# One convolution pair in every slot, the first six in the slots of the image two ahead, in a two-layer convolution kernel

## The chip, the cores and the metric

The kernel runs on one core of one Trainium2 chip. The metric is the device time of the whole program in microseconds (us), the median of several executions. PE is TensorE, DVE is VectorE, ACT is ScalarE, POOL is GpSimd, SP is SyncE, which here only issues DMAs.

## The reference

The input x has 32 images of 16 channels and 256 x 256 points, in fp32. Two residual layers follow each other, each with a group normalisation (8 groups of 2 channels) ahead of it:

```
x = x + conv3x3_int8(group_norm(x))          # layer 0
x = x + irfft2(conv3x3_complex(rfft2(group_norm(x))))   # layer 1
```

Layer 0 scales the normalised input by the largest absolute value of the *whole* batch over 128, rounds it, clips it to +-127, convolves it with 16 x 16 x 3 x 3 integer weights, scales back and adds a bias. Layer 1 takes a real 2-D FFT, convolves the spectrum with complex 3 x 3 weights, adds a complex bias, and transforms back.

## The kernel before

A first pass reads all images and takes the statistics of the first normalisation and the batch's maximum. Then comes the main part, image by image. An image stands in SBUF as 128 partitions (16 channels by 8 rows) by 32 row blocks by 256 columns, in one of two buffers: `img[u]`, u the image's parity. Its 32 row blocks are 16 *pairs*.

**The order of the work is written out by hand.** Every engine has a function `period`, which runs for one image s and goes through 16 *slots*, t = 0 to 15. In slot t the engines finish pair t of image s, and do earlier stages of later pairs. `periods` (line 308) calls `period` for all images, with three flags: `mix` (image s is being finished), `conv` (image s + 1 is in layer 0), `ahead` (there is an image s + 2). What belongs to which slot:

- **PE** (`period`, line 1079): `turn_pair(t+4)` transposes the folded rows (L963), `dft_pair(t+3)` transforms them (L972), `mix_pair(t+1)` multiplies with the weights (L985, 48 matmuls), `finish_pair(t)` transforms back (L999 to L1004). Beside these it has layer 0 of image s + 1: `conv_pair` (three matmuls on the quantised rows, L1017, and one on the halo rows, L1019) and `row_means` of the pair before (L1030). `CONV_OF` (line 38) says which convolution pairs are in which slot: one in slots 0 to 3, two in slots 4 to 9 (the second one behind `mix_pair`), none in slots 10 to 15. Slot 10 has `group_stat` twice (L1046), for mean and variance of the second normalisation of image s + 1; slots 12 to 15 have small steps with its row means (`centre_rows`, `dft_rows`, `mix_rows`, `finish_rows`).
- **DVE** (line 905), in this order: `y_low(t)` (L827), `stats_mean` in slot 10 (L855, L857), `stats_out` in slot 11 (to L877), `x_low(t+3)` (L821), `layer0_pair` (the residual add L834 and its statistics L836), `stats_var` in slot 10 (L864 to L870), `round_pair` (L813, L815), `layer0_pair` of a second pair, `finish_pair(t)` (four adds, L844 to L849).
- **ACT** (line 564): `turn_out(t+4)` (L540), `x_high(t+3)` (L547), `scale_pair` (L533), `y_high(t+1)` (L554), and the store of pair t - 2 (L562).
- **POOL**: `fold(t+4)` (L729 to L732), which from slot 12 on is that of image s + 1 and needs its statistics.
- **SP** (line 457): in slot t it waits for the store of pair t - 3 and loads that pair of image s + 2 (`load_pair`, L376), waits for `x_low(t+3)` and the mixing of pair t + 1 and copies the result into shifted rows for PE (`restack`, L454, four DMAs), and in slots 2, 6, 10 and 14 copies halo rows of a quarter image out of the quantised rows (`halo_rows`, L443, two DMAs).

`AHEAD` = 10 says how far `scale_pair` and `round_pair` are ahead: in slot t they have pair t + 10 of image s + 1, from slot 6 on pair t - 6 of image s + 2 (`quant_of`, line 304). A convolution pair waits for the rounding of its whole quarter image (four pairs) and for the halo copies of it. `conv_ps`, where the convolution goes, has one buffer: `conv_pair` waits until DVE has added the pair before (`x1_s`).

```
dve.wait_ge(conv_s, m + 1 + PAIRS)
nc.vector.scalar_tensor_tensor(rows, conv_ps[:], out_scale, rows, ALU.mult, ALU.add).then_inc(x1_s, 1)
```

Ahead of the first image, ACT and DVE scale and round ten pairs of image 0, SP copies two quarters of halos, and one period with s = -1 runs the whole of layer 0 of image 0 (the *lead-in*).

## Time and profile before

| | |
|---|---|
| median of 3 runs | 3781.86 us (3779.63 to 3790.49) |
| the profiled execution | 3767.42 us |
| its span, first to last instruction | 3765.6 us |
| mean granted PE clock in it | 0.992 |
| images 0 to 29, 696.36 to 3604.45 us of the span | 2908.09 us, 96.94 each |
| period of image 30 | 93.91 us |

A period is counted from the first transposes of its slot 0 on PE to those of the next one. PE's matmuls overlap, so a row's duration is longer than the distance to the next row's start; distances between starts are what PE needs.

### The profile page before, as it was taken

The numbers are of one execution on the slowest core, as the hardware profiler recorded it, in microseconds if no ns is written. First come the engines' busy times: TensorE is split into PE (matmuls) and PEld (weight loads), VectorE is DVE, ScalarE is ACT, GpSimd is POOL, SyncE is SP. The second block draws the span as 40 slices with busy tenths as digits, with TensorE's granted clock in tenths as the row PEclk, the third lists the DMA queues.
The fourth block names the chain that finished last, engine by engine and source line by source line (L and its number), as shares of the span: only waits on it lengthen the run. The fifth ranks groups of instructions, "written<-read, shape, count | busy, mean of one in ns | idle before, by whom it ended". The sixth has DMA issues, their size and how long they took to land.

```text
span 3765.6 us, 126495 instructions
## 1 busy us (share of the span) xinstructions
PE 2979.5 (79%) x45732; PEld 2646.9 (70%) x45732; DVE 3117.7 (83%) x5880; ACT 1893.1 (50%) x2799; POOL 1490.4 (40%) x1984
## 2 busy tenths in 40 slices
PE   0000004899999999999999989999999999999998
PEld 0000002788888888888888878888888888888888
DVE  8999994688878888888888878888888888888876
ACT  8999981344444444444444434444444444444443
POOL 4777000344334344343343334333433433333444
PEclk9999999999999999999999999999999999999999
DMA  8767650366666666666666656666666666666655
GB/s 309 241 236 242 236 188 16 118 196 198 198 188 196 197 195 197 194 192 195 199 194 191 195 178 194 194 192 195 192 194 191 196 192 194 193 199 191 198 179 179
DMA packets 630696, 730.98 MB, mean 194 GB/s; under 512 B 76752, under 2 KB 602160, under 8 KB 614736
## 3 DMA queue, kind: packets, MB, share of 16 engines
q1 hardware_dynamic: 482640, 588.71, 48.6%
q10 hardware_dynamic: 147456, 134.28, 12.7%
q8 instruction: 374, 6.13, 0.7%
q14 instruction: 226, 1.85, 0.2%
HBM read 262.58 MB, written 134.22 MB: 105 GB/s over the span
## 4 chain that ended last, share of the span: by engine, by line
PE 50%; SPq 16%; issue 11%; DMA 11%; DVE 9%; ACT 1%; POOL 1%; ACTq 1%; DVEq 0%; POOLq 0%
PE y_ps L985 12%; PE mean_b L1030 10%; SPq L454 9%; PE conv_ps L1017 7%; PE x_ps L972 6%; DMA stack<-xn 5%; PE fin_ps L1004 5%; SPq L376 4%; PE t_ps L963 3%; DMA out<-img 3%; PE conv_ps L1019 3%; DVE scaled L758 2%; DMA img<-in_x 2%; PE fin_ps L999 2%; DVE scaled L759 1%
## 5 line engine op out<-in xcount | busy, mean ns | idle before, releaser
L729 POOL TENSOR_SCALAR eo<-img,norm 128x256 f32<-128x256 f32 x512 | 481.5, 940 | 1502.1 <-PE t_ps L963 1274.2
L985 PEld LDWEIGHTS y_ps<-mix_w,stack 128*128 128x128 f16 x24576 | 787.5, 99 | 158.1 <-DMA stack<-xn 84.6
L985 PE MATMUL y_ps<-mix_w,stack 128*128 128x64 f16 x24576 | 810.4, 194 | 62.4 <-DMA stack<-xn 62.0
L540 ACT ACTIVATE xt<-t_ps 128x512 f32<-128x512 f32 x512 | 305.8, 597 | 910.8 <-PE t_ps L963 802.9
L554 ACT ACTIVATE y_hi<-y_ps 128x512 f16<-128x512 f32 x512 | 305.8, 597 | 535.4 <-PE y_ps L985 534.4
L834 DVE SCALAR_TENSOR_TENSOR img<-conv_ps,cst,img 128x512 f32<-128x512 f32 x512 | 382.3, 747 | 226.9 <-PE conv_ps L1019 226.4
L821 DVE SCALAR_TENSOR_TENSOR xn<-x_ps,norm,xn 128x512 f16<-128x512 f32 x512 | 383.1, 748 | 220.7 <-ACT xn L547 215.6
L1030 PE MATMUL mean_b<-row_mean,img 128*128 128x48 f32 x4096 | 538.2, 275 | 16.6 <-DVE img L834 16.2
L972 PE MATMUL x_ps<-dft,xt 128*128 128x128 f32 x4096 | 543.0, 276 | 0.0
L1030 PEld LDWEIGHTS mean_b<-row_mean,img 128*128 128x128 f32 x4096 | 511.3, 196 | 31.7 <-DVE img L834 31.5
L972 PEld LDWEIGHTS x_ps<-dft,xt 128*128 128x128 f32 x4096 | 499.7, 192 | 0.1
L547 ACT ACTIVATE xn<-x_ps,norm 128x512 f16<-128x512 f32 x512 | 352.4, 688 | 231.0 <-DMA stack<-xn 145.3
L533 ACT ACTIVATE scaled<-img,b,a 128x512 f32<-128x512 f32 x512 | 412.0, 805 | 106.1 <-DVE quant L813 71.1
L1004 PE MATMUL fin_ps<-inv,y_hi 128*128 128x128 f16 x4096 | 459.1, 221 | 0.0
L951 PE MATMUL misc_ps<-im_f,group 128*128 128x32 f32 x2 | 0.6, 396 | 575.5 <-DVE im_f L779 575.5
L1017 PE MATMUL conv_ps<-quant,conv_w 128*128 128x512 bf16 x1536 | 427.2, 388 | 25.6 <-DMA halo<-quant 25.5
L951 PEld LDWEIGHTS misc_ps<-im_f,group 128*128 128x128 f32 x2 | 0.5, 310 | 575.5 <-issue 575.5
L1004 PE MATMUL fin_ps<-inv,y_lo 128*128 128x128 f16 x2048 | 400.6, 221 | 0.0
L1004 PEld LDWEIGHTS fin_ps<-inv,y_hi 128*128 128x128 f16 x4096 | 358.8, 99 | 39.6 <-issue 0.2
L730 POOL TENSOR_TENSOR eo<-img 128x256 f32<-128x256 f32 x512 | 381.1, 744 | 0.0
L732 POOL TENSOR_TENSOR eo<-eo,img 128x256 f32<-128x256 f32 x512 | 376.2, 735 | 0.0
L836 DVE BATCH_NORM_STATS2 bn<-img 128x6 f32<-128x512 f32 x512 | 355.6, 694 | 17.6
(134 smaller groups left out, 5138.9 us busy)
## 6 DMA issues: line engine op xcount, KB each, us to landing
stack<-xn SPq DMA_DIRECT2D x2048, 132.0 KB, 2.6
img<-in_x SPq DMA_DIRECT2D x1024, 128.0 KB, 2.8
out<-img ACTq DMA_DIRECT2D x1024, 128.0 KB, 3.0
img<-in_x SPq DMA_DIRECT2D x120, 1024.0 KB, 4.9
halo<-quant SPq DMA_DIRECT2D x192, 193.3 KB, 3.3
halo<-quant SPq DMA_DIRECT2D x64, 169.1 KB, 3.0
row_mean<-table_row_mean SPq DMA_DIRECT2D x1, 768.0 KB, 15.4
spread<-table_spread SPq DMA_DIRECT2D x1, 512.0 KB, 14.4
```

The source lines that it names most:

```text
L533: nc.scalar.activation(scaled[:], img[u][:, 2 * j:2 * j + 2, :], ACT.Identity, bias=b0[:, bass.ds(k, 1)], scale=a0[:, bass.ds(k, 1)]).then ...
L729: nc.gpsimd.tensor_scalar(even, rows[:, :, 0:F], norm[v][:, 2:3], None, ALU.add).then_inc(shift_s, 1)
L730: nc.gpsimd.tensor_tensor(odd, rows[:, :, 0:F], rows[:, :, N - 1:F - 1:-1], ALU.subtract)
L732: nc.gpsimd.tensor_tensor(even, even, rows[:, :, N - 1:F - 1:-1], ALU.add).then_inc(fold_s, 1)
L821: nc.vector.scalar_tensor_tensor(natural(t, 1), x_ps[:].rearrange("p q b k -> p (q b) k"), norm[v][:, 4:5], natural(t, 0), ALU.mult, ALU.s ...
L834: nc.vector.scalar_tensor_tensor(rows, conv_ps[:], out_scale, rows, ALU.mult, ALU.add).then_inc(x1_s, 1)
L836: nc.vector.bn_stats(bn[:, c, :], rows).then_inc(bn_s, 1)
L972: last = nc.tensor.matmul(x_ps[:, q, b, :], xt[:, t % 2, b, q, :], dft[:, q, :], start=True, stop=True)
L985: last = nc.tensor.matmul(y_ps[t % 2][:, g, b, :], stack[:, t % 2, g, first:first + F], mix_w[:, 2 * at + b, g, f, part, :], start=i == 0, ...
L1004: last = nc.tensor.matmul(fin_ps[:, b, q, :], y[:, t % 2, 2 * b + q].rearrange("p x g -> p (x g)"), inv[:, q, part, :], start=False, stop= ...
L1017: nc.tensor.matmul(conv_ps[:], conv0_w[:, dw, :], quant[:, 2 * c:2 * c + 2, dw:dw + N], start=dw == 0, stop=False)
L1030: nc.tensor.matmul(mean_ps[half], img[u][:, hb, F * half:F * half + F], row_mean[:, hb, :], start=False, stop=False)
```

## The change

Every slot gets one convolution pair. In slots 0 to 9 it is pair t + 6 of image s + 1, in slots 10 to 15 pair t - 10 of image s + 2. It always stands ahead of `mix_pair`; on DVE `layer0_pair` stands ahead of `stats_var` and of the rounding. Row means follow a list of their own, `MEANS_OF`: slots 14, 15 and 0 have two pairs, slots 1 to 10 one, slots 11 to 13 none, because the accumulator is in use until slot 12. Scaling and rounding are 12 pairs ahead. ACT stores pair t - 1 rather than t - 2, SP loads pair t - 2 rather than t - 3. SP's halo copies are in slots 0, 4, 8 and 12 and come first in the slot. The lead-in has no steps of its own any more: a further period with s = -2 does the first roundings and convolutions of image 0.

```diff
--- before.py
+++ after.py
@@ -35,11 +35,12 @@
 STORES = 4
 NQ = 8
 
-CONV_OF = [[j] if j < 4 else [2 * j - 4, 2 * j - 3] if j < 10 else [] for j in range(PAIRS)]
 BOUND = 5
 STATS_AT = 10
 IMAGE_AT = 12
-AHEAD = 10
+AHEAD = 12
+CONV_LEAD = 6
+MEANS_OF = {14: (0, 1), 15: (2, 3), 0: (4, 5), **{t: (t + 5,) for t in range(1, 11)}}
 TERMS = [(0, 0, 0), (0, 0, 2), (1, 0, 1), (0, 1, 1), (1, 1, 0), (1, 1, 2)]
 TABLES = ("dft", "dft_back", "channel", "ident", "inv", "row_mean", "spread", "first_row", "pulse", "group", "mask", "wave_k", "coef_m", "coef_i")
 
@@ -305,8 +306,17 @@
 
             return (1, j + AHEAD) if j < PAIRS - AHEAD else (2, j - PAIRS + AHEAD)
 
+        def conv_of(t):
+
+            return (1, t + CONV_LEAD) if t < PAIRS - CONV_LEAD else (2, t - PAIRS + CONV_LEAD)
+
+        def means_of(t):
+
+            return (2 if t >= PAIRS - 2 else 1), MEANS_OF.get(t, ())
+
         def periods(engine, period):
 
+            period(-1, 0, False, False, True)
             period(-1, 1, False, True, True)
             rounds = (SP2 - 1 - PEEL) // TURN
             for v in range(PEEL):
@@ -457,20 +467,20 @@
             def period(i, u, mix, conv, ahead):
                 s = 2 * i + u
                 for t in range(PAIRS):
-                    if mix and t >= 3 and ahead:
-                        sp.wait_ge(store_s[(t - 3) % STORES], stored(s, t - 3))
+                    if t in (0, 4) and conv:
+                        halo_rows(s + 1, t // 4 + 2)
+                    if t in (8, 12) and ahead:
+                        halo_rows(s + 2, t // 4 - 2)
+                    if mix and t >= 2 and ahead:
+                        sp.wait_ge(store_s[(t - 2) % STORES], stored(s, t - 2))
                         sp.sem_inc(tick_s, 1)
-                        load_pair(s + 2, u, t - 3)
-                    if later(s, mix) and t < 3 and conv:
-                        sp.wait_ge(store_s[(t - 3) % STORES], stored(s - 1, t + PAIRS - 3))
+                        load_pair(s + 2, u, t - 2)
+                    if later(s, mix) and t < 2 and conv:
+                        sp.wait_ge(store_s[(t - 2) % STORES], stored(s - 1, t + PAIRS - 2))
                         sp.sem_inc(tick_s, 1)
-                        load_pair(s + 1, 1 - u, t + PAIRS - 3)
+                        load_pair(s + 1, 1 - u, t + PAIRS - 2)
                     if runs(mix, conv, t + 3):
                         restack(s, t + 3)
-                    if t in (2, 6) and conv:
-                        halo_rows(s + 1, t // 4 + 2)
-                    if t in (10, 14) and ahead:
-                        halo_rows(s + 2, t // 4 - 2)
 
             for u in range(2):
                 for q in range(QU):
@@ -483,8 +493,6 @@
             for u in range(2):
                 for j in range(PAIRS):
                     sp.sem_inc(pair_s[u][j], 1)
-            for c in range(2):
-                halo_rows(0, c)
             periods(sp, period)
             for b in range(STORES):
                 sp.wait_ge(store_s[b], 32 * PAIRS // STORES * samples + 1)
@@ -589,17 +597,14 @@
                         act.wait_ge(imps_s, s + 2)
                         nc.scalar.activation(im_f[:, 0:F], image_ps[:, 0, :], ACT.Identity, bias=image_b)
                         nc.scalar.activation(im_f[:, F:N], image_ps[:, 1, :], ACT.Copy).then_inc(imf_s, 1)
-                    if mix and t >= 2:
-                        store(s, u, t - 2)
-                    if later(s, mix) and t < 2:
-                        store(s - 1, 1 - u, t + PAIRS - 2)
+                    if mix and t >= 1:
+                        store(s, u, t - 1)
+                    if later(s, mix) and t == 0:
+                        store(s - 1, 1 - u, PAIRS - 1)
 
             act.wait_ge(scale_s, 1)
-            for j in range(AHEAD):
-                scale_pair(0, 0, j)
             periods(act, period)
-            for t in (PAIRS - 2, PAIRS - 1):
-                store(samples - 1, 1, t)
+            store(samples - 1, 1, PAIRS - 1)
 
 
         @block.gpsimd
@@ -905,7 +910,6 @@
             def period(i, u, mix, conv, ahead):
                 s = 2 * i + u
                 for t in range(PAIRS):
-                    pairs = CONV_OF[t] if conv else []
                     if mix:
                         y_low(s, t)
                     if mix and t == 0:
@@ -920,23 +924,20 @@
                         x_low(s, u, t + 3)
                     if conv and t == IMAGE_AT + 3:
                         iy_low(s + 1)
-                    if pairs:
-                        layer0_pair(s + 1, 1 - u, pairs[0])
+                    d, c = conv_of(t)
+                    if conv if d == 1 else ahead:
+                        layer0_pair(s + d, (u + d) % 2, c)
                     if conv and t == STATS_AT:
                         stats_var(s + 1)
                     if conv if t < PAIRS - AHEAD else ahead:
                         d, jq = quant_of(t)
-                        round_pair(s + d, jq, not mix and d == 1)
-                    for c in pairs[1:]:
-                        layer0_pair(s + 1, 1 - u, c)
+                        round_pair(s + d, jq, isinstance(i, int) and s + d == 0)
                     if mix:
                         finish_pair(s, u, t)
                     if conv and t == IMAGE_AT + 3:
                         images_first(s + 1)
 
             dve.wait_ge(weights_1, HB + 1)
-            for j in range(AHEAD):
-                round_pair(0, j, True)
             periods(dve, period)
 
 
@@ -1079,27 +1080,25 @@
             def period(i, u, mix, conv, ahead):
                 s = 2 * i + u
                 for t in range(PAIRS):
-                    pairs = CONV_OF[t] if conv else []
                     if runs(mix, conv, t + 4):
                         turn_pair(s, t + 4)
                     if runs(mix, conv, t + 3):
                         dft_pair(s, t + 3)
-                    if conv and t == STATS_AT:
-                        row_means(s + 1, 1 - u, PAIRS - 1)
-                        group_stat(s + 1, meane_s, 0, gmean_s)
                     if conv and t == IMAGE_AT:
                         centre_rows(s + 1, 1 - u)
-                    for c in pairs[:1]:
-                        if c:
-                            row_means(s + 1, 1 - u, c - 1)
-                        conv_pair(s + 1, c)
+                    d, means = means_of(t)
+                    if conv if d == 1 else ahead:
+                        for c in means:
+                            row_means(s + d, (u + d) % 2, c)
+                    if conv and t == STATS_AT:
+                        group_stat(s + 1, meane_s, 0, gmean_s)
+                    d, c = conv_of(t)
+                    if conv if d == 1 else ahead:
+                        conv_pair(s + d, c)
                     if conv and t == IMAGE_AT + 2:
                         mix_rows(s + 1)
                     if runs(mix, conv, t + 1):
                         mix_pair(s, t + 1)
-                    for c in pairs[1:]:
-                        row_means(s + 1, 1 - u, c - 1)
-                        conv_pair(s + 1, c)
                     if conv and t == STATS_AT:
                         group_stat(s + 1, e_s, 1, gvar_s)
                     if mix:
```

## Rows read from the trace of the kernel before

**Rows 1.** The page, busy time of each engine over the whole span.

```profile
PE 2979.5 (79%) x45732; PEld 2646.9 (70%) x45732; DVE 3117.7 (83%) x5880; ACT 1893.1 (50%) x2799; POOL 1490.4 (40%) x1984
```

**Rows 2.** Windows; columns: window, its us, busy us per engine, clock, DMA share, GB/s.

```profile
696.36:3604.45 2908.09, 2758.89 (x42874) 2463.08 (x42871) 2388.33 (x5248) 1269.62 (x2100) 1151.27 (x1470) 0.99 0.63 194
3604.45:3698.36 93.91, 90.77 (x1432) 81.37 (x1430) 72.71 (x156) 35.62 (x60) 37.67 (x49) 1.00 0.53 163
2652.53:2657.85 5.32, 5.32 (x90) 4.82 (x87) 5.25 (x12) 2.58 (x4) 2.30 (x3) 1.00 0.68 209
2664.95:2672.04 7.09, 7.09 (x101) 6.11 (x99) 6.09 (x13) 2.58 (x4) 2.30 (x3) 1.00 0.60 188
2700.43:2707.08 6.65, 5.53 (x94) 5.38 (x91) 5.16 (x16) 2.58 (x4) 0.40 (x1) 1.00 0.38 120
2707.08:2712.52 5.44, 3.79 (x78) 3.58 (x75) 5.24 (x18) 2.51 (x4) 3.09 (x5) 1.00 0.80 229
2014.93:2022.98 8.05, 6.93 (x93) 6.68 (x91) 5.50 (x17) 2.58 (x4) 0.85 (x1) 0.81 0.43 131
```

**Rows 3.** Timeline of PE in slot 3 of an image; columns: start, us, engine, line.

```profile
2652.53 0.60 PE L963 MATMUL t_ps<-ident,eo 128*128 128x128 f32 x4
2652.97 1.06 PE L972 MATMUL x_ps<-dft,xt 128*128 128x128 f32 x8
2653.86 0.99 PE L1030 MATMUL mean_b<-row_mean,img 128*128 128x48 f32 x8
2654.69 0.81 PE L1017 MATMUL conv_ps<-quant,conv_w 128*128 128x512 bf16 x3
...
2655.56 1.56 PE L985 MATMUL y_ps<-mix_w,stack 128*128 128x64 f16 x48
```

**Rows 4.** Timeline of PE, then of DVE, in slots 10 and 11 of the same image.

```profile
2703.88 0.61 PE L1046 MATMUL misc_ps<-small,group 128*128 128x1 f32 x4 [1.12 <-DVE small L857]
2704.35 1.56 PE L985 MATMUL y_ps<-mix_w,stack 128*128 128x64 f16 x48
2705.74 0.58 PE L1046 MATMUL misc_ps<-small,group 128*128 128x1 f32 x4
...
2712.52 0.66 PE L963 MATMUL t_ps<-ident,eo 128*128 128x128 f32 x4 [1.65 <-POOL eo L732]
...
2699.74 0.75 DVE L834 SCALAR_TENSOR_TENSOR img<-conv_ps,cst,img 128x512 f32<-128x512 f32 x1 [0.99 <-PE conv_ps L1019]
...
2701.14 0.41 DVE L844 SCALAR_TENSOR_TENSOR img<-fin_ps,img 128x256 f32<-128x256 f32 x1
...
2704.60 0.16 DVE L864 COPY small<-misc_ps 128x2 f32<-128x2 f32 x1
...
2704.99 0.22 DVE L866 SCALAR_TENSOR_TENSOR small<-small 128x1 f32<-128x1 f32 x1
...
2706.44 0.16 DVE L870 TENSOR_SCALAR small<-misc_ps 128x2 f32<-128x2 f32 x1 [1.16 <-PE misc_ps L1046]
```

**Rows 5.** Waits over the span (total us, times, longest); then SP's timeline, slots 14 and 15.

```profile
PEld y_ps L985 <- DMA stack<-xn: 84.6, 83, 2.5
...
2731.43 1.85 SPq L443 DMA_DIRECT2D halo<-quant  x2
2733.64 1.64 SPq L376 DMA_DIRECT2D img<-in_x  x2
2735.53 2.69 SPq L454 DMA_DIRECT2D stack<-xn  x4
```

**Rows 6.** DVE timeline by slot 3; then line L815 (duration ns min/median/max).

```profile
2653.04 0.41 DVE L813 TENSOR_SCALAR quant<-scaled 128x512 bf16<-128x512 f32 x1
...
2657.85 0.41 DVE L813 TENSOR_SCALAR quant<-scaled 128x512 bf16<-128x512 f32 x1
...
L815 DVE TENSOR_SCALAR quant<-quant x512: 298/301/711, 592.5 to 3638.6; 128x512 bf16<-128x512 bf16 x171
```

**Rows 7.** Windows, columns as in rows 2: one convolution pair of the lead-in.

```profile
615.58:620.07 4.49, 3.65 (x13) 2.18 (x13) 2.07 (x5) 0.81 (x1) 0.00 (x0) 1.00 0.00 0
```

## The prediction

> **What bounds the kernel now.** I first read the busy shares of the page [rows 1]: TensorE (PE) 79% and VectorE (DVE) 83% of the span. These are means over a statistics pass, a lead-in and 32 image periods, so next I cut the main part into windows [rows 2]. Images 0 to 29 take 2908.09 us, 96.94 us each, with PE busy in 2758.89 of them. Within an image the slots differ. Slot 3 (one convolution pair) takes 5.32 us, PE busy in all of it. Slot 5 (two pairs) takes 7.09 us, again with PE busy throughout. Slot 10 (none) takes 6.65 us with 5.53 busy, slot 11 (none) 5.44 with 3.79 busy. So PE is the limit while it holds convolutions, and other things set the pace in slots that have none.
>
> The timeline of slot 3 gives the prices, as distances between starts [rows 3]: transposes 0.44, forward DFT 0.89, row means 0.83, one convolution pair 0.87, mixing from 2655.56, which with the inverse transform makes the remaining 2.29. These add up to the 5.32 of the window, so nothing is lost there. Without convolution and means a slot is 3.62 us of PE. Slot 5 is 5.32 plus 1.77 for a second pair and its means.
>
> PE's losses per image are four. In slot 10 it has 0.44 + 0.89 + 0.83 = 2.16 us of work and would start the group matmul at 2702.59; it starts at 2703.88, held by the mean of the statistics [rows 4]: 1.29 us (the row's own figure is 1.12; a stop costs PE 0.17 more than it shows, as the matmuls no longer overlap). Slot 11 takes 5.44 instead of 3.62: 1.82 us, nearly all of it POOL's fold for the next image's first transposes, which start at 2712.52. Waits for the restacking DMAs are 84.6 us at the weight loads, in 83 stops [rows 5]: with 0.17 for each, (84.6 + 14)/31 = 3.2 us per image. And in some images the granted clock falls in slot 10: such a slot took 8.05 us at a mean clock of 0.81, so part of it at 1.2 GHz, against 6.65 at 1.00 [rows 2], 1.40 us more. As the mean over images 0 to 29 rounds to 0.99, I put it at 0.5 us per image.
>
> **The change, part by part.** *PE's work is moved, not removed*: 16 pairs and 16 row means per image as before. Only the losses, some 6.8 us, can be won.
>
> *Slots 1 to 9* become nine slots of the pattern of slot 3, 5.32 us each. That they can follow one another at this pace hangs on DVE. Around slot 3 it goes from one rounding to the next in 2657.85 - 2653.04 = 4.81 us [rows 6], so at least 0.5 us of a slot is left to it. These slots should lose nothing, as now.
>
> *Slots 12 to 15 and 0* get 0.87 us for a pair each; 14, 15 and 0 hold two row means (0.83 each) too. The restack waits are there today, because PE runs through light slots faster than the chain from DVE's low part over SP's four DMAs back to PE. With the chain unchanged and each of these slots 0.9 to 2.5 us longer, I take 3.2 down to 0.4: **-2.8 us per image.** The nearest rows are slots 3 and 5 themselves, with PE busy in all of the window; so the bounds are 0 left, and all 3.2 left if light slots aren't the cause.
>
> *Slots 10 and 11* take a pair of the image two ahead. The mean: today DVE has a second layer-0 add from 2699.74, so its finishing adds begin at 2701.14, 0.71 after PE ended slot 9 at 2700.43; 2.74 us later, at 2703.88, PE has the mean [rows 4]. With slot 9's one pair ahead of the mixing, the adds can begin some 0.2 after the slot's start, my estimate of the hand-over. The group matmul then starts at 0.2 + 2.74 = 2.94 of the slot, after 2.16 of work: a wait of 0.8 instead of 1.29. The variance: the new layer-0 step stands before it on DVE. From the group matmul's start, 0.47 (four matmuls, as the mixing row shows: 2704.35 - 2703.88) and the pair's 0.87 end at 4.28. DVE follows 0.2 later with add and statistics, 1.40 (2699.74 to 2701.14), then copy, difference and square, 0.61 (2704.60 to the end of L866). The second group matmul can start at 6.5, while mixing (1.40 = 2705.74 - 2704.35) ends at 5.7: **a new wait of 0.8 us**, with the matmul and the inverse transform queued behind it on PE. From that matmul to L870 is 0.70 us, from L870 to the next image's transposes 2712.52 - 2706.44 = 6.08 [rows 4]: these start at 6.5 + 6.8 = 13.3. Slots 10 and 11 together are 13.3 us instead of 12.09: 1.2 longer for 1.74 of moved work, so **-0.5 us per image**. The clock: two shorter stops instead of 1.29 and 1.82, I take **-0.2**.
>
> *SP's queue.* The halo copies move ahead of load and restack. In the trace the three take 1.85, 1.64 and 2.69 us of issue [rows 5], 6.2 us in one turn of four, 4.3 in the others: 19.1 us for four slots of at least 5.0. SP keeps up. The halo's wait for the rounding of the slot before costs nothing: DVE rounds soon after the low part that SP's last restack needed, while SP still issues it. Without this cover every instruction queued behind (store wait, load, restack) is late. The load moves up one slot with the store, so their distance is unchanged; from load to scaling two slots remain of three, still over 9 us. At nothing.
>
> *ScalarE's store* moves up a slot and waits for DVE's finishing adds of the slot before. These are done some 1.5 us into the slot, the store comes after y_high, over 4 us into it. Nothing; if DVE were late, the next eviction of the transposes would stand behind it.
>
> *Per image* -2.8 - 0.5 - 0.2 = **-3.5 us, for 30 images -105.**
>
> *Ends.* Image 30's period (93.91 us [rows 2]) loses six pairs and four row means: 6 x 0.87 + 4 x 0.83 = 8.5 us less. The lead-in takes them on. There one pair with its mean takes 4.49 us, PE busy in 3.65 of it [rows 7]. Bounds for the added work: 0, if it falls into waits; 6 x 4.49 = 27, if it goes as slowly as that and hides nowhere. Against it stand about 4 us, as the first pairs no longer wait for ten roundings. I take 9 - 4 = +5. Together -3.5.
>
> Total -108.5. The profiled execution took 3767.42 us (span 3765.6), 0.4% under the median of 3781.86; I expect 3659 for a profile and **3673 us** as the median.
>
> **Two rules of the Trainium skill.** In the Trainium skill, Perfetto Trace Analysis (Identifying the Most-Contended Engine) says that matmul busy time misleads and weight-load busy time measures TensorE's room. That is 4.82 of 5.32 us in slot 3, so by the rule nine slots could give 4.5 us per image more; but the starts in slot 3 show no gap, and I add nothing. In the Trainium skill, SBUF — State Buffer (Who interferes with whom) says that GpSimd and a two-port DVE operation block each other; rival B has its row.
>
> **Rivals.**
> **A: the new stop in slot 10 pulls the clock down in every image.** For it: it fell to a mean of 0.81 in one such slot, and there will be two stops with one-column matmuls beside them. Against: each is shorter than 1.29. Price 1.4 instead of 0.3, 1.1 x 30 = 33: **3706**.
> **B: DVE sets the pace of the equal slots.** Its second rounding step takes 298 ns at the least and 711 at the most [rows 6]. At 0.7 in each slot DVE needs up to 4.81 + 0.4 = 5.2, and with two hand-overs of 0.2 in a slot 5.6: 0.28 x 9 = 2.5 per image, 75: **3748**. Against: POOL's fold starts after the transposes and is done before the rounding in even slots.
> **C: the restack waits don't come from light slots** but from DMA traffic or SP's order. Then 2.8 per image stay, 84: **3757**.
> **D, slower than before: halo copies first hold up SP.** If SP is there before DVE has rounded, load and restack are late and PE stops at the mixing two slots on. It decides from 3.5/4 = 0.9 us per halo slot. At 1.5: 6.0 - 3.5 = +2.5 per image, and with the ends 3782 + 75 - 4 = **3853**. Against: the cover named above.
> **E: it does nothing**: the chain over DVE, ACT and SP has the same mean pace either way, and what one slot gains the next waits for: **3780**.
>
> **Chances.** Forecast 0.54, A 0.15, B 0.12, C 0.09, D 0.06, E 0.04. The range takes in the forecast (lead-in 0 to 27, and on the good side all restack, clock and mean waits gone, (0.4 + 0.3 + 0.5) x 30 = 36), A and most of B: 3635 to 3745. Under 0.3% (11 us) a measurement can't tell from no change. Faster 0.90, same 0.04, slower 0.06.
>
> **What the profile should show.** Slots 1 to 9 at 5.32 us; slots 10 and 11 together near 13.3, with a new PE wait for DVE L866 near 0.8; a wait for the fold near 0.9; PE's waits for restacks under 15 us in all. I am wrong in the main point if the nine slots are over 5.4, or if restack waits stay.

## The result, and the profile after

The changed kernel took 3692.11 us (median, 3688.6 to 3694.08) against 3786.18 us (3779.63 to 3794.59) for the one before: a ratio of 0.9749, 95% interval 0.9726 to 0.9773. 3673 was forecast, in a range of 3635 to 3745. The profiled execution's span went from 3765.6 to 3686.8 us, 78.8 less. That is less than the 94 us of the medians, because the profiled execution of before (3767.42) was 19 us under its median, and that of after (3688.6) 3.5 us. One of the six executions of a kernel below (restack first) took 4771.82 us at a mean granted clock of 0.756; its ratio leaves that one out.

The page of the changed kernel, busy time by engine (it answers to [rows 1]):

```profile
PE 2952.2 (80%) x45732; PEld 2630.6 (71%) x45732; DVE 3147.2 (85%) x5880; ACT 1888.0 (51%) x2799; POOL 1481.3 (40%) x1984
```

Windows of the changed kernel, columns as in [rows 2]: images 0 to 29, image 30, then slots 3, 5, 10, 11 and 13 of image 14:

```profile
700.28:3536.77 2836.49, 2734.43 (x42873) 2449.55 (x42871) 2416.81 (x5249) 1265.11 (x2101) 1142.42 (x1470) 0.99 0.65 199
3536.77:3620.46 83.69, 81.78 (x1375) 75.25 (x1372) 65.11 (x141) 34.00 (x58) 37.65 (x49) 1.00 0.56 173
2030.61:2035.93 5.32, 5.32 (x90) 4.82 (x87) 4.84 (x11) 2.58 (x4) 2.30 (x3) 1.00 0.64 203
2041.25:2048.58 7.33, 5.49 (x90) 4.89 (x87) 4.99 (x11) 2.58 (x4) 2.29 (x3) 1.00 0.70 199
2069.86:2077.75 7.89, 6.58 (x97) 5.83 (x95) 6.02 (x17) 2.58 (x4) 0.39 (x1) 1.00 0.63 190
2077.75:2082.82 5.07, 4.66 (x82) 3.98 (x79) 4.88 (x13) 2.58 (x4) 2.92 (x5) 1.00 0.62 190
2087.74:2094.13 6.39, 5.77 (x89) 4.79 (x87) 6.03 (x15) 2.64 (x6) 2.30 (x3) 1.00 0.72 220
```

An image takes 2836.49/30 = 94.55 us, 2.39 less than the 96.94 of before, where 3.5 less was forecast. Slot 3 is as dense as forecast. But slot 5, which has the same work, takes 7.33 us with PE busy in 5.49. The waits of the changed kernel (total us, times, longest us), against [rows 5]:

```profile
PE conv_ps L1018 <- DMA halo<-quant: 72.3, 42, 23.2
PE misc_ps L1047 <- DVE small L871: 22.7, 29, 2.1
PE misc_ps L1047 <- DVE small L862: 20.9, 31, 1.3
PE t_ps L964 <- POOL eo L737: 15.5, 31, 2.6
PEld y_ps L986 <- DMA stack<-xn: 6.0, 7, 2.3
```

The restack waits are all but gone, from 84.6 us in 83 stops to 6.0 in 7. In their place PE waits for the halo copies: 72.3 us, of which 23.2 is the start of the lead-in, as before, and 49.1 us in 41 stops come after it (2.3 us in 6 stops before). One of the 41 is still in the lead-in; the others, counted in the trace, are in slot 5 (20 stops) and slot 13 (20) of images 0 to 29. Where a slot's median is given below, it is over images 1 to 29.

### The profile page after: what moved, and what is told of

It is laid out like the page before. It is cut to its first block, busy times and chain, and to the rows that moved or that the text cites. A ratio compares the mean times of both kernels' runs of the same rounds, so it can differ in the third digit from the quotient of the medians.

```text
span 3686.8 us, 126585 instructions
## 1 busy us (share of the span) xinstructions
PE 2952.2 (80%) x45732; PEld 2630.6 (71%) x45732; DVE 3147.2 (85%) x5880; ACT 1888.0 (51%) x2799; POOL 1481.3 (40%) x1984
## 4 chain that ended last, share of the span: by engine, by line
PE 54%; SPq 13%; DMA 11%; issue 11%; DVE 7%; ACTq 1%; ACT 1%; POOL 1%; DVEq 0%; POOLq 0%
PE y_ps L986 14%; PE mean_b L1031 9%; PE x_ps L973 7%; PE conv_ps L1018 7%; SPq L464 7%; PE fin_ps L1005 6%; DMA halo<-quant 4%; DMA out<-img 4%; PE t_ps L964 4%; SPq L386 3%; PE conv_ps L1020 2%; DVE scaled L763 2%; DMA img<-in_x 2%; PE fin_ps L1000 2%; DVE scaled L764 1%
## 5 line engine op out<-in xcount | busy, mean ns | idle before, releaser
L1031 PE MATMUL mean_b<-row_mean,img 128*128 128x48 f32 x4096 | 512.8, 273 | 8.4 <-DVE img L839 8.4
L1018 PE MATMUL conv_ps<-quant,conv_w 128*128 128x512 bf16 x1536 | 429.9, 390 | 74.5 <-DMA halo<-quant 72.3
## 6 DMA issues: line engine op xcount, KB each, us to landing
spread<-table_spread SPq DMA_DIRECT2D x1, 512.0 KB, 14.6
```

The costliest lines, as they stand in the source:

```text
L1018: nc.tensor.matmul(conv_ps[:], conv0_w[:, dw, :], quant[:, 2 * c:2 * c + 2, dw:dw + N], start=dw == 0, stop=False)
L1031: nc.tensor.matmul(mean_ps[half], img[u][:, hb, F * half:F * half + F], row_mean[:, hb, :], start=False, stop=False)
```

## The experiments

Twelve kernels were run beside the change, one of them the change again. Each ratio is to the kernel before on the same chip. Before itself took 3786 to 3788 us on the other chips, but 3769 on that of the two early-store kernels and of the change again, so kernels of different chips are compared by ratio. By ratio, the intervals of load one slot later, restack first, restack first with the stats split, and early store overlap: the table alone doesn't rank these four.

| kernel | median us | ratio to before, 95% interval |
|---|---|---|
| the change | 3692.11 | 0.9749 (0.9726 to 0.9773) |
| halo copies last | 4337.83 | 1.1458 (1.1424 to 1.1491) |
| rounding 13 ahead | 3707.32 | 0.9789 (0.9770 to 0.9808) |
| load one slot later | 3663.47 | 0.9676 (0.9657 to 0.9695) |
| before, queues only | 3784.95 | 1.0001 (0.9985 to 1.0017) |
| stats split | 3707.43 | 0.9799 (0.9772 to 0.9827) |
| thin convolution (one run) | 3613.56 | none |
| restack first | 3665.24 | 0.9674 (0.9650 to 0.9698) |
| restack first, stats split | 3657.61 | 0.9654 (0.9628 to 0.9679) |
| early store | 3641.48 | 0.9659 (0.9633 to 0.9684) |
| early store, stats split | 3624.94 | 0.9610 (0.9582 to 0.9637) |
| the change again | 3678.55 | 0.9764 (0.9737 to 0.9790) |
| before, early store | 3756.30 | 0.9912 (0.9893 to 0.9931) |

### Did the light slots cause the restack waits?

Before with SP's, ACT's and the rounding's part of the change alone; the convolutions stay at one, two and none per slot:

```diff
-AHEAD = 10
+AHEAD = 12
...
+                    if t in (0, 4) and conv:
+                        halo_rows(s + 1, t // 4 + 2)
+                    if t in (8, 12) and ahead:
+                        halo_rows(s + 2, t // 4 - 2)
...
-                        load_pair(s + 2, u, t - 3)
+                        load_pair(s + 2, u, t - 2)
...
-                    if t in (2, 6) and conv:
-                        halo_rows(s + 1, t // 4 + 2)
-                    if t in (10, 14) and ahead:
-                        halo_rows(s + 2, t // 4 - 2)
...
-                        store(s, u, t - 2)
+                        store(s, u, t - 1)
```

> The kernel before, with its convolutions as they were (one, two and none per slot), and only the queues moved as in the change: scaling and rounding 12 ahead, store and load one slot earlier, halo copies first in slots 0, 4, 8 and 12. The forecast's reason (light slots cause the restack waits): these stay at 2 to 3 us per image, and the time stays within 20 us of before, about 3786. Rival C turned round (SP's order did it): restack waits go without the convolutions moving, and the time falls to 3690 to 3720.

Its waits for the restack:

```profile
PEld y_ps L984 <- DMA stack<-xn: 106.5, 99, 2.7
```

They rose from 84.6 to 106.5 us, and the time did not change. So SP's order by itself did not take the restack waits away; what the change has beyond this kernel is the place of the convolutions (with DVE's steps for them). A kernel with the convolutions moved and the queues left was not run. Rival C is out, and E is by the result itself.

Where the waits were before tells more (PE's own, at the matmuls, counted by slot in images 0 to 30): 36.0 us in slots 13, 15 and 0, and 21.2 us in slots 1 to 3, which have the same work before and after. The likeliest reading is that the chain was still behind in slots 1 to 3, after the light ones, and that levelling slots 12 to 0 took these waits away too.

### Is it the halo copies' lateness that costs?

```diff
-                    if t in (0, 4) and conv:
-                        halo_rows(s + 1, t // 4 + 2)
-                    if t in (8, 12) and ahead:
-                        halo_rows(s + 2, t // 4 - 2)
...
                         restack(s, t + 3)
+                    if t in (0, 4) and conv:
+                        halo_rows(s + 1, t // 4 + 2)
+                    if t in (8, 12) and ahead:
+                        halo_rows(s + 2, t // 4 - 2)
```

> The changed kernel with SP's halo copies last in slots 0, 4, 8 and 12 instead of first; all else as after. Theory 1 (the halo copies reach their convolution pair too late, and that is the 1.6 us per image that the forecast missed): they come about 4 us later, behind one load and one restack, so PE's halo waits in slots 5 and 13 grow by about 4 us each and one appears in slot 1: 8 to 11 us more per image, 30 x 8 = 240 us or more slower than after, about 3930 us or above, slower than before. Rival (the halo wait only takes the place of another wait, the chain per image stays): within 30 us of after, about 3690 to 3720.

The waits and the window of images 0 to 29:

```profile
PE conv_ps L1018 <- DMA halo<-quant: 530.4, 99, 23.2
```

```profile
701.83:4169.92 3468.09, 2921.16 (x42873) 2570.13 (x42871) 2420.78 (x5249) 1264.02 (x2101) 1142.87 (x1470) 0.91 0.53 163
```

Three slots, 1, 5 and 13, now take a median of 12.4, 12.1 and 13.7 us, with a stop in each in every image, and the image 115.6. Theory 1 has the direction right and the size far too small: 8 to 11 us more per image were expected, 21 came. In slot 4 of image 14 (it begins at 2346.16) the copies go here:

```profile
2356.47 1.22 SPq L453 DMA_DIRECT2D halo<-quant  x2
```

That is 10.3 us after the slot's start, where the change has 4.2: some 6 us later, not 4. And the mean granted clock was 0.924 instead of 0.995, which comes on top of the missed time. The place of these two DMAs in SP's queue decides over hundreds of microseconds.

### Why are they late? SP's queue

SP's timeline in the changed kernel, slots 3 and 4 of image 14, with ScalarE's stores of the same stretch below:

```profile
2035.02 2.06 SPq L386 DMA_DIRECT2D img<-in_x  x2
2037.33 2.58 SPq L464 DMA_DIRECT2D stack<-xn  x4
2040.11 1.22 SPq L453 DMA_DIRECT2D halo<-quant  x2
2041.58 2.54 SPq L386 DMA_DIRECT2D img<-in_x  x2
...
2035.45 1.60 ACTq L570 DMA_DIRECT2D out<-img  x2
2040.76 1.40 ACTq L570 DMA_DIRECT2D out<-img  x2
```

PE needed the copies for slot 5's convolution. By the starts of [rows 3] it stands 0.44 + 0.89 + 0.83 = 2.16 behind the slot's start, 2041.25, so it would have started at 2043.4; it started at 2045.42:

```profile
2045.42 0.81 PE L1018 MATMUL conv_ps<-quant,conv_w 128*128 128x512 bf16 x3 [1.84 <-DMA halo<-quant]
```

Mixing ended at 2035.0, so the restack could have gone then. It went at 2037.33, as the load ahead of it, released only at 2035.02, had waited for a store issued in the slot before. The halo copies went at 2040.11, behind the restack, though DVE had finished the rounding that they need at 2035.98 (its row of line 820, from 2035.68, lasts 0.30): 4.1 us in which only SP's own queue held them. Each store is issued with y_high, at the end of mixing, and SP stands at its landing until the mixing of the next slot ends. SP's waits (total us, times, longest us):

```profile
SPq L476 <- DMA out<-img: 187.5, 176, 3.4
SPq L480 <- DMA out<-img: 38.9, 41, 2.3
```

Four edits move this. **Load one slot later** gives a store a slot more to land:

```diff
-                    if mix and t >= 2 and ahead:
-                        sp.wait_ge(store_s[(t - 2) % STORES], stored(s, t - 2))
+                    if mix and t >= 3 and ahead:
+                        sp.wait_ge(store_s[(t - 3) % STORES], stored(s, t - 3))
...
-                        load_pair(s + 2, u, t - 2)
+                        load_pair(s + 2, u, t - 3)
```

> The changed kernel with SP's load of a pair one slot later again (pair t - 3), while ScalarE's store stays one slot earlier, so that SP has a slot more between store and load. Theory 2 (SP comes late to the halo because the load before it waits for the store: 187.5 us of SP's waits): SP's wait for out<-img goes to near 0, the halo copies are issued about 2 us earlier, PE's halo waits go, about 3640 us. Rival (the copies are late by the rounding or by their own landing time): SP waits elsewhere and the halo waits stay, 3685 to 3700 us.

SP's waits for stores vanished but for the last ones, and the halo waits fell to 35.9 - 23.1 = 12.8 us. Yet the time fell by less than forecast: slot 10 went from 7.89 to a median of 8.55. Two rows of this kernel show where it went:

```profile
ACT scaled L541 <- DMA img<-in_x: 168.9, 130, 3.8
PE misc_ps L1047 <- DVE small L862: 35.1, 31, 2.3
```

The pair now comes one slot before it is scaled. ScalarE waits for it, most of all in slots 5 (37.0 us) and 9 (50.6 us, counted in the trace), one slot behind the halo copies that stand ahead of the load. DVE's rounding waits for ScalarE, and DVE's finishing adds in slot 9 start a mean of 0.74 us after PE's end instead of 0.24. In slot 10, PE waits for DVE's mean, and pays. Two images of this trace show the link: in image 1 ScalarE scales 3.01 us into slot 9, DVE rounds at 4.63 and slot 10 takes 7.88; in image 9 it scales at 4.67, DVE rounds at 5.52 and slot 10 takes 8.55.

**Rounding 13 pairs ahead** lets the copies go a slot earlier:

```diff
-AHEAD = 12
+AHEAD = 13
...
-                    if t in (0, 4) and conv:
-                        halo_rows(s + 1, t // 4 + 2)
-                    if t in (8, 12) and ahead:
-                        halo_rows(s + 2, t // 4 - 2)
+                    if t == 15 and ahead:
+                        halo_rows(s + 2, 2)
+                    if t == 3 and conv:
+                        halo_rows(s + 1, 3)
+                    if t in (7, 11) and ahead:
+                        halo_rows(s + 2, t // 4 - 1)
```

> The changed kernel with scaling and rounding 13 pairs ahead and the halo copies first in slots 15, 3, 7 and 11, one slot earlier. Theory 1: PE's waits for the halo (1.6 us shown per image, 1.8 with the refill) go, the rest stays: 30 x 1.8 = 54 us, about 3638 us; slots 5 and 13 at 5.3 and 5.5. Rival (SP is the limit of the slots now, and the halo wait was just where it showed): waits for the restack come in its place, and the time stays at 3680 to 3700.

Neither theory had the outcome, 15 us slower than the change in the medians. The halo waits did go (only the lead-in's is left), restack waits of PE were 14.6 us, and the loss had a third place:

```profile
ACT scaled L543 <- DMA img<-in_x: 510.4, 300, 4.4
PE misc_ps L1049 <- DVE small L864: 54.2, 31, 2.7
PE conv_ps L1020 <- DMA halo<-quant: 23.3, 1, 23.3
```

```profile
2073.20:2083.91 10.71, 7.96 (x97) 7.03 (x95) 7.17 (x20) 3.88 (x6) 0.40 (x1) 0.84 0.51 156
```

The last is its slot 10 in image 14, 10.7 us with the clock at a mean of 0.84. The pair again comes one slot before it is scaled, but here its load also still waits for the store (151.8 us of SP's waits), and ScalarE waits three times as long as in the run before.

**Restack first, load last** in SP's slot:

```diff
+                    if runs(mix, conv, t + 3):
+                        restack(s, t + 3)
+                    if t == 3 and conv:
+                        halo_rows(s + 1, 3)
+                    if t in (7, 11, 15) and ahead:
+                        halo_rows(s + 2, t // 4 - 1)
                     if mix and t >= 2 and ahead:
...
-                    if runs(mix, conv, t + 3):
-                        restack(s, t + 3)
```

> The changed kernel with SP's order in a slot turned round: restack, then halo copies (slots 3, 7, 11 and 15, behind the rounding of the same slot), then the load. Nothing else moves; rounding stays 12 ahead and the load keeps its slot. Theory (SP is late for the halo because load and restack of the slot before stand behind a store's landing): the load finds its store landed, SP's wait for out<-img falls from 226 us to under 60, the halo copies are issued 2 to 2.5 us earlier, PE's halo waits go but for a few, ScalarE's scaling does not wait for the load as it did with a margin of one slot, slot 10 stays at 7.9: 1.8 us per image, about 3638 us, and below the 3663 of the run with the later load. Rival (without the stops in slots 5 and 13 DVE falls behind and slot 10 takes it back, as in the two runs before): slot 10 at 8.5 or more, 3660 us.

Here too the halo waits went (38.5 - 23.2 = 15.3 us) and ScalarE waited for loads (193.8 us), and 3665 us came out: the rival's number. I had thought that a margin of nearly two slots would do.

**The store ahead of y_high** frees SP without making any load later:

```diff
+                    if mix and t >= 1:
+                        store(s, u, t - 1)
+                    if later(s, mix) and t == 0:
+                        store(s - 1, 1 - u, PAIRS - 1)
                     if runs(mix, conv, t + 1):
                         y_high(s, t + 1)
...
-                    if mix and t >= 1:
-                        store(s, u, t - 1)
-                    if later(s, mix) and t == 0:
-                        store(s - 1, 1 - u, PAIRS - 1)
```

> The changed kernel with ScalarE's store of pair t - 1 ahead of y_high in the slot, not behind it; nothing on SP is moved. The store is issued about 2.4 us earlier, when DVE's finishing adds are done (1.6 us into the slot) and ScalarE would only wait for the mixing. Theory (the store's landing holds SP's load, the load holds restack and halo copies, and the halo copies hold PE): SP's wait for out<-img falls from 226 us to about 100 or less, as SP comes to it earlier or finds it landed; halo copies 2 us earlier; PE's halo waits (49 us without the first) go below 15; ScalarE's scaling does not wait for the load (that cost DVE's pace in the runs with the later load); about 3640 us, the best of the single edits. Rival (without the halo stops slot 10 takes the time back, whatever the load does): 3660 to 3665 as in the runs with the later load and with the restack first.

> The changed kernel as it is, once more, beside the two above on the same chip: 3692 us within 6, PE's halo waits 45 to 55 us without the first one. It tells how far the others may be set against the runs of the first job.

The change again took 3678.55 us, not 3692, with 40.1 us of halo waits: both outside what I had put down. Its ratio, 0.9764, agrees with the first one's 0.9749. The early store took 3641.48 us, 37 less than the change on the same chip. SP in slots 3 and 4 of its image 14 (slot 4 begins at 2026.02):

```profile
2023.44 1.50 SPq L386 DMA_DIRECT2D img<-in_x  x2
2025.52 2.99 SPq L464 DMA_DIRECT2D stack<-xn  x4
2028.70 1.23 SPq L453 DMA_DIRECT2D halo<-quant  x2
2030.19 1.35 SPq L386 DMA_DIRECT2D img<-in_x  x2
```

The halo copies go 2.7 us after the start of slot 4; in the change it was 2040.11 - 2035.93 = 4.2 us. SP's waits for stores inside the images and PE's halo waits:

```profile
SPq L476 <- DMA out<-img: 0.2, 1, 0.2
...
PE conv_ps L1018 <- DMA halo<-quant: 43.6, 26, 23.1
```

As in the change, and unlike the last three kernels, ScalarE has no wait for a pair to be scaled among its larger ones; DVE's adds in slot 9 start 0.2 us after PE's end, and slot 10 stays at 7.89. The halo waits are 20.5 us after the first, a little above the 15 that I had put down; most of them are in slot 13. That this edit beats load later and restack first in time is not shown, as its ratio lies within their intervals; what it has for itself is that slot 10 pays nothing.

### The new wait in slot 10

```diff
                 ch.link(nc.vector.tensor_tensor(z_tmp, bias2, g_mean, ALU.subtract))
+
+            def stats_eps(k):
+
                 dve.wait_ge(gvar_s, k + 1)
...
+                    if conv and t == STATS_AT:
+                        stats_var(s + 1)
                     d, c = conv_of(t)
                     if conv if d == 1 else ahead:
                         layer0_pair(s + d, (u + d) % 2, c)
                     if conv and t == STATS_AT:
-                        stats_var(s + 1)
+                        stats_eps(s + 1)
```

> The changed kernel with one step moved on DVE: the copy, difference and square of stats_var stand before the layer-0 step of slot 10 again, and only the last one, which needs the second group matmul (now stats_eps), behind it. Theory (the wait for DVE L871 in slot 10, 0.8 us per image, is the price of the layer-0 step standing ahead of stats_var): it goes, slots 10 and 11 fall from 12.96 to 12.2 or 12.5 us, 15 to 24 us in all, about 3670 us. Rival (the chain that ends in the fold of the next image decides, and it only moves its wait from slot 10 to the transposes of slot 12): under 0.1 us per image, 3688 to 3692.

Slot 10 fell from 7.89 to 7.03 us (medians), as the price said, and the kernel was no faster than the change: its ratio is 0.9799 against 0.9749 and 0.9764, and the intervals of the first and the last overlap, so that it was slower is likely but not sure. The 0.86 us came back as halo waits:

```profile
PE conv_ps L1023 <- DMA halo<-quant: 102.1, 53, 23.3
```

That is 78.8 us after the first, against 49.1. Slot 13's median went from 6.24 to 7.04. A shorter slot 10 brings the convolution of slot 13 nearer to halo copies that come when they come. With the queue mended, the gain shows. The same split, put on restack first:

> Both edits together: SP's order turned round and stats_var split. If the two losses are independent, the gains add: 1.8 + 0.6 per image, about 3620 us. If the chain from DVE's lag into slot 10 decides once the halo waits are gone, the split brings nothing on top: the same as the run with SP's order alone, within 5 us.

And put on the early store:

> The early store and the split stats_var together. Alone, the split made slot 10 0.86 us shorter and the kernel 15 us slower, as slots 10 to 12 then run up against the halo copies of slot 12. Theory: with the copies 2 us earlier its gain shows, 0.5 to 0.8 us per image below the early store alone, about 3620 us. Rival (slot 13 still waits for the halo): at most 8 us below the early store alone, as it was with the restack first.

On top of restack first it gave 8 us in the medians, with intervals that overlap, so nothing clear of noise and not the 3620 of added gains; on top of the early store 16.5 us, 3624.94 in all, the quickest kernel of the study, 54 us under the change on the same chip. Its images 0 to 29 and slots 10 and 13 of one image:

```profile
698.76:3474.49 2775.73, 2715.34 (x42874) 2436.21 (x42871) 2431.31 (x5249) 1283.50 (x2101) 1142.78 (x1470) 1.00 0.66 203
2046.51:2053.53 7.02, 6.39 (x97) 5.76 (x95) 6.14 (x18) 2.58 (x4) 0.47 (x1) 1.00 0.70 217
2063.50:2070.23 6.73, 5.76 (x89) 4.79 (x86) 6.03 (x15) 2.70 (x6) 2.30 (x3) 1.00 0.81 254
```

That is 2775.73/30 = 92.52 us per image, against 94.55 in the change and 96.94 before, though slot 13, with PE busy in 5.76 of 6.73 us, still waits for its halo copies.

### What bounds the equal slots?

```diff
-                for dw in range(3):
+                for dw in range(1):
```

> The changed kernel with one of the three matmuls on the quantised rows per convolution pair left in (columns dw = 1 and 2 of the 3 x 3 weights are left out; the halo matmul stays). PE has 0.43 us less work per pair. If PE is the bound of the equal slots, slots 1 to 9 fall from 5.32 to 4.89 us, and the image by 16 x 0.43 = 6.9 us. If DVE is close behind (rival B), they stop between: its work is at most 4.8 us of a slot with hand-overs of 0.2, so some 5.0 to 5.1 us, and the image by 3 to 4 us.

Two thirds of the convolution's matmuls on the quantised rows are left out here. Slot 3, then slot 10:

```profile
1990.98:1995.86 4.88, 4.88 (x87) 4.62 (x85) 4.69 (x11) 2.58 (x4) 2.31 (x3) 1.00 0.68 216
2027.58:2035.91 8.33, 6.14 (x96) 5.63 (x93) 7.00 (x19) 2.58 (x4) 0.40 (x1) 1.00 0.68 213
```

The equal slots fell to 4.89 us (median): PE sets their pace in the change, not DVE; rival B is out. But the image fell only to 92.6, by 2.0 of the 6.9 us. Slot 5 went to 7.8 and slot 10 to 8.6, since the halo copies and the statistics don't come sooner when PE is quicker. And with shorter slots the restack waits came back, which the change had at 4.4 us in 4 stops:

```profile
PE y_ps L986 <- DMA stack<-xn: 24.7, 29, 2.4
```

This is one run, but it speaks for the forecast's reason from the other side: where PE's slot gets shorter than the chain over DVE and SP, PE stops for the restack.

### Would the early store alone have done it?

Before, with ScalarE's stores ahead of `y_high` and nothing else:

```diff
+                    if mix and t >= 2:
+                        store(s, u, t - 2)
+                    if later(s, mix) and t < 2:
+                        store(s - 1, 1 - u, t + PAIRS - 2)
                     if runs(mix, conv, t + 1):
                         y_high(s, t + 1)
...
-                    if mix and t >= 2:
-                        store(s, u, t - 2)
-                    if later(s, mix) and t < 2:
-                        store(s - 1, 1 - u, t + PAIRS - 2)
```

> The kernel BEFORE with one edit: ScalarE's store (of pair t - 2) ahead of y_high. Convolutions, rounding and SP's order stay as they were. Theory 3 (the restack waits of the light slots come from SP, which stands at the landing of a store, some 4.9 us after the mixing, before it loads and restacks; a slot of 3.6 to 4 us is shorter than that): PE's restack waits fall from 62 us to below 20, and the time by 60 to 80 us, to 0.98 of before, so that equal slots were one way to hide the store's landing and not the only one. Rival (the light slots themselves, through DVE and the four DMAs, with or without the load): restack waits stay at 50 us or more, the time within 15 us of before.

The restack waits at PE's matmuls, then SP's waits for stores, each in the kernel before and in this one:

```profile
PE y_ps L985 <- DMA stack<-xn: 62.0, 68, 2.4
PE y_ps L985 <- DMA stack<-xn: 52.9, 56, 2.5
...
SPq L462 <- DMA out<-img: 166.9, 161, 2.9
SPq L462 <- DMA out<-img: 6.5, 9, 1.4
```

SP's wait for stores in the images fell from 166.9 to 6.5 us, but PE's restack waits at the matmuls themselves (the 84.6 of [rows 5] are those at the weight loads) only from 62.0 to 52.9: the rival is right on the waits, and the store's landing is not what made them. The rival is wrong on the time: the median fell by 32 us, not by 15 at most, and the interval is clear of 1. The restack waits show 9 of them; where the others come from stays open, as the one profile's span fell by 6 us only.

## Why the prediction was right, and where it was short

**Direction and size were right**, the median 19 us above the forecast, the profiled execution (3688.6 against 3659) 30 above. By steps:

*Restack waits, -2.8 us per image.* Measured 3.2 to 0.2, -3.0 (the same sum: 6.0 us and 7 stops). The two controls on the kernel before show that neither SP's order nor the store's landing did it, and the thin convolution brings the waits back. Of the slots I had named, 12 to 15 and 0, they held only part: over a third of the waits was in slots 1 to 3.

*Slots 1 to 9 at 5.32.* All but slot 5: medians of 5.32.

*Slots 10 and 11, 13.3 us, with a new wait.* Measured 7.89 + 5.07 = 12.96. The stops in image 14 of the change:

```profile
2072.82 0.61 PE L1047 MATMUL misc_ps<-small,group 128*128 128x1 f32 x4 [0.63 <-DVE small L862]
...
2076.40 0.61 PE L1047 MATMUL misc_ps<-small,group 128*128 128x1 f32 x4 [0.68 <-DVE small L871]
...
2082.82 0.66 PE L964 MATMUL t_ps<-ident,eo 128*128 128x128 f32 x4 [0.41 <-POOL eo L737]
```

The group matmuls start at 2.96 and 6.54 of the slot (2069.86), 2.94 and 6.5 were worked out, and the transposes at 12.96, against 13.3. The fold is where the 0.3 was gained: its wait was 15.5/31 = 0.5 us, not 0.9.

*The clock, -0.2.* Its mean rose from 0.992 to 0.995. Counted in the traces, it fell 17 times before, 11 of them in slot 10, and 9 times in the change, 2 in slot 10 and 6 in slot 5, where the new halo stop is. Slot 10's mean was 0.56 us above its median before (7.21 and 6.65) and 0.17 in the change (8.06 and 7.89): about -0.4 us per image. Rival A did not come.

*SP's queue, "at nothing": this step failed.* I added up SP's issue times and concluded that it keeps up. It does, but keeping up is about the mean, and the halo copies have a deadline. I had SP restack as mixing ends, and so reach the halo copies 2.6 us later, with DVE's rounding as the only other condition. In fact the load ahead of the restack stood at a store's landing, the restack went 2.3 us later and the copies with it. I had written down that the distance from store to load was unchanged, and this was true; that it was already too short, and would now stand in front of something urgent, is what I missed. With the 0.17 that a stop costs beyond what its row shows (slot 5 is 7.33 - 5.32 = 2.01 for a stop of 1.84), it cost (49.1 + 41 x 0.17)/31 = 1.8 us per image. The sum closes: -3.0 for the restack, -0.9 for slots 10 and 11 (1.74 us of moved work for 12.96 - 12.09 = 0.87), -0.4 for the clock and + 1.8 give -2.5, and -2.39 was measured.

*Luck.* The failed term alone is 30 x 1.8 = 54 us. That the profile missed by 30 only is because the other terms came out better than forecast, by 0.2 (restack), 0.4 (slots 10 and 11) and 0.2 us (clock) per image and by 3.7 at the ends. Nothing in the forecast foresaw that they would make good half of it. The range's lower end doesn't follow from its own terms either: with the lead-in at 0 and 36 us won it is 3673 - 9 - 36 = 3628, not 3635.

*Rival D* had the right queue and the wrong victim. It had SP held at the halo copies and the restack late, which was to cost more than the change won from 0.9 us per halo slot on. It was the copies that were late, by other instructions of the queue. The kernel with the copies last shows how near the other side is: the same edit with the copies behind one restack and one load is 15% slower than before.

*The ends, -3.5.* Image 30 fell by 93.91 - 83.69 = 10.2 us (8.5 forecast), the first image began 700.28 - 696.36 = 3.9 later (5 forecast), the last part was 0.9 shorter: -7.2. With 30 x -2.39 = -71.6, that makes the 78.8 us of the spans.

**The two rules cited.** By the Trainium skill, Perfetto Trace Analysis (Identifying the Most-Contended Engine), weight-load busy time tells PE's room, which would be 9% in the equal slots (4.82 of 5.32 us busy). With two matmuls per pair left out they got 0.43 us shorter while weight-load busy time fell by 0.20 only (to 4.62), so here the starts of the matmuls, and not the weight loads, tell whether PE is full. What the Trainium skill, SBUF — State Buffer (Who interferes with whom), says of GpSimd and DVE did not bear on the time: DVE's second rounding step has a median of 0.30 us in the changed kernel, and the equal slots stayed at 5.32.

## What to carry to other kernels

Levelling the work of the busiest engine over the slots of a hand-written schedule takes away waits which a longer chain causes in and just after the light slots, even where the engine is busy 95% of the time; but every transfer's deadline moves with the slots. For each transfer that is moved, work out when its queue reaches it (what stands before it, and what that waits for), not only whether the queue keeps up on average. Where a queue waits for a store's landing, try first to bring the store forward: it cost nothing elsewhere here, while the load, moved behind the urgent work or made later, missed its own reader. On time alone the single edits are not clearly apart; the early store with the split is clear of the load later and of restack first.

## What the runs showed that I had not expected

In the kernels with the load later or last, late loads don't stop PE in their own slot: slots 6 to 9 stay at 5.32 us. (With rounding 13 ahead the medians do too, but PE has 14.6 us of restack waits.) They delay ScalarE, and DVE behind it: its finishing adds of slot 9 start 0.74 to 1.40 us after PE's end (means of load later and rounding 13 ahead), and that is paid in slot 10, where PE needs DVE's newest result. In load later, lateness in slots 5 and 6 is made up before that (0.22 us is left in slot 7); what counts is the load of slot 8. So a wait of PE that is named for a DVE instruction had a DMA two slots back as its cause, over two other engines.

With three stops of 5 to 6 us per image the mean granted clock was 0.924, against 0.995 in the change. With two stops of 0.6 to 0.7 us in slot 10 and few others it was 0.998 in the kernel with the early store, and 0.992 before, with a stop of 1.1 and one of 1.65 us.
